# A decoder layer's cross-attention: exponentials of the second half per bank, one maximum over it, and probabilities kept as half-precision bit patterns

## The reference, cut to what matters

```python
q = (x @ Wq + bq).reshape(1, B * N, H, hd)          # 1024 queries
kv = (cond @ Wkv + bkv).reshape(1, -1, 2, H, hd)    # 2048 keys
k, v = (kv[:, :, 0], kv[:, :, 1])
...
q = _fq_sym(q, axis=-1)
k = _fq_sym(k, axis=-1)
v = _fq_sym(v, axis=2)
attn = jnp.einsum('bhqd,bhkd->bhqk', q, k)
attn = jax.nn.softmax(attn.astype(jnp.float32), axis=-1)
attn = _fq_unsigned(attn, axis=-1)    # step = row maximum / 255, rounded to 0..255 steps
out = jnp.einsum('bhqk,bhkd->bhqd', attn, v)
out = jnp.transpose(out, (0, 2, 1, 3)).reshape(B, N, C)
return out @ Wp + bp
```

## Time and profile before

| what | value |
|---|---|
| median of 3 runs | 1241.23 us (1237.27 to 1243.06) |
| the profiled execution, its own time | 1237.78 us |
| span of the profiled execution | 1236.1 us |
| `cross_scores`, first score matmul to last output copy | 399 to 871 us |
| busy over the whole span | PE 81%, DVE 69%, ACT 57%, POOL 20% |
| granted PE clock over the span | 0.95 of full speed |
| DMA inside `cross_scores` | nearly none: 0 to 3 GB/s in most slices |

### The profile page before, as it was taken

How to read it: one execution, slowest core, us unless ns; L and a number is a source line. 1 busy time by engine, 2 the same in 40 slices (tenths; PEclk the granted TensorE clock), 3 DMA queues, 4 the chain that set the end, 5 groups by cost and what they waited for, 6 DMA issues and landing times. The chain is left out here.

```text
span 1236.1 us, 21867 instructions
## 1 busy us (share of the span) xinstructions
PE 1003.9 (81%) x8049; PEld 682.7 (55%) x8049; DVE 852.8 (69%) x1409; ACT 700.4 (57%) x1039; POOL 243.6 (20%) x216
## 2 busy tenths in 40 slices
PE   4888996999457777777777777777779989999998
PEld 3745744888345444444444444444557765556566
DVE  6857546999687899999999999999661521111126
ACT  3453362455426899999999999999223202212221
POOL 1134063556250200000000000000533610000014
PEclk9999998999678799999999999999779989999999
DMA  8200004110000000000000000000040395131215
GB/s 320 96 1 1 1 2 154 51 34 17 9 0 13 31 1 2 1 0 0 0 0 0 0 0 0 0 0 0 1 151 27 135 379 230 60 116 64 69 56 182
DMA packets 24854, 68.14 MB, mean 55 GB/s; under 512 B 2722, under 2 KB 6818, under 8 KB 23778
## 3 DMA queue, kind: packets, MB, share of 16 engines
q1 hardware_dynamic: 20114, 52.48, 11.3%
q0 software_dynamic: 4400, 14.42, 3.7%
q10 hardware_dynamic: 288, 0.52, 0.1%
HBM read 49.07 MB, written 18.35 MB: 55 GB/s over the span
## 5 line engine op out<-in xcount | busy, mean ns | idle before, releaser
L1313 DVE TENSOR_REDUCE cs_top<-cs_s_b 128x1 f32<-128x512 f32 x256 | 164.8, 685 | 16.7 <-PE cs_s_b L1342 7.6
L1350 PE MATMUL cs_tp<-ident,cs_p_int 128*128 128x128 f16 x2048 | 158.4, 221 | 7.5 <-ACT cs_pT L1293 2.8
L1287 ACT ACTIVATE cs_p_int<-cs_s_b,cs_bias,cs_step_now 128x1024 int16<-128x1024 f32 x128 | 154.1, 1204 | 11.6 <-DVE cs_bias L1320 5.3
L1301 DVE TENSOR_REDUCE cs_top<-cs_s_a 128x1 f32<-128x1024 f32 x128 | 155.5, 1215 | 7.2 <-PE cs_s_a L1342 7.2
L1350 PEld LDWEIGHTS cs_tp<-ident,cs_p_int 128*128 128x128 f16 x2048 | 122.1, 98 | 60.3 <-issue 45.6
L1342 PE MATMUL cs_s_b<-k_parts,q_int 96*128 96x512 bf16 x256 | 79.0, 391 | 93.4 <-ACT cs_p_int L1287 93.1
L1287 ACT ACTIVATE cs_p_int<-cs_s_a,cs_bias,cs_step_now 128x1024 int16<-128x1024 f32 x128 | 152.8, 1194 | 0.0
L1293 ACT CAST cs_pT<-cs_tp 128x1024 bf16<-128x1024 int16 x128 | 129.5, 1012 | 3.3 <-PE cs_tp L1350 2.7
L2159 PE MATMUL ff_h<-ff_experts,ff_zgT 128*128 x368 | 115.1, 467 | 1.0 <-ACT ff_zgT L1798 0.9
L1446 POOL TENSOR_TENSOR co_o<-co_o,v_step 128x512 f32<-128x512 f32 x8 | 10.7, 1331 | 467.6 <-DVE co_o L1468 467.6
L1342 PE MATMUL cs_s_a<-k_parts,q_int 96*128 96x512 bf16 x256 | 79.4, 393 | 22.9 <-ACT cs_p_int L1287 18.7
(11 more groups left out here) (278 smaller groups left out, 2099.0 us busy)
## 6 DMA issues: line engine op xcount, KB each, us to landing
ff_experts<-in_experts_dram SPq DMA_DIRECT2D x8, 2176.0 KB, 14.6
slots<-sa_zero SPq DMA_DIRECT2D x1, 5888.0 KB, 25.8
ff_zg<-slots POOLq DMA_DIRECT2D x23, 256.0 KB, 2.9
run_y<-ff_yv SPq DMA_DIRECT2D x23, 256.0 KB, 2.0
ff_raw<-in_weights_dram SPq DMA_DIRECT2D x6, 768.0 KB, 5.8
ck_raw<-in_ctxT_dram SPq DMA_DIRECT2D x8, 512.0 KB, 3.3
stage<-in_cwkv_dram SPq DMA_DIRECT2D x2, 1024.0 KB, 6.8
out_dram<-x_res SPq DMA_DIRECT2D x8, 256.0 KB, 2.0
```

Of the source, the lines that this page charges most:

```text
L1287: nc.scalar.activation(p_int[:, u, half * HALF:(half + 1) * HALF], s[:, :], ACT.Exp, bias=bias[:, u:u + 1], scale=step_now[:, h:h + 1], ac ...
L1301: nc.vector.tensor_reduce(top[:, u, 0:1], s_a[u][:, :], AX_X, ALU.max).then_inc(max_ok, 1)
L1313: nc.vector.tensor_reduce(top[:, u, 1 + c:2 + c], s_b[:, c * 512:(c + 1) * 512], AX_X, ALU.max).then_inc(max_ok, 1)
L1350: ins = nc.tensor.transpose(tp[:, k, :], p_int[:, u, key:key + P].bitcast(F16), ident16[:, :])
```

## The change

It has five parts.

1. The exponential of half b is issued as two instructions of 512 keys, one for each bank (`PIECES = 3` sums per head instead of 2), and `eb_ok` is counted up by each. PE's score matmul for the first bank of the next unit waits for the first of them, that for the second bank for the second.
2. The maximum of half b is one instruction over 1024 values behind both score matmuls, in place of two instructions of 512, each behind its own.
3. The transposed probabilities stay bit patterns: `cs_pT` is int16, and L1376 (L1380 now) reads them as float16, in which the integer n is the subnormal number n * 2^-24. `v_int` becomes float16, and the copy of the output multiplies by 2^24 (`P_UNIT`).
4. ACT copies half b in pairs, as 512 int32 values instead of 1024 int16 ones. A pair is at most 255 * 65536 + 255, below 2^24. DVE copies half a as 1024 int16 values as before, to int16.
5. One exponential of a single column (`table`) stands ahead of the units on ACT.

The second score matmul now has a wait of its own. The diff, without the new declarations of constants and tiles that repeat part 3:

```diff
+            nc.scalar.activation(table[:, :], ident16[:, 0:1], ACT.Exp)
             units(act, step)
...
-                for half, s, made, used in ((1, s_b, eb_ok, tb_ok), (0, s_a[u], ea_ok, ta_ok)):
-                    if half:
+                for i, (first, count, s, made, used) in enumerate(((HALF, 512, s_b[:, 0:512], eb_ok, tb_ok),
+                                                                   (HALF + 512, 512, s_b[:, 512:HALF], eb_ok, None),
+                                                                   (0, HALF, s_a[u][:, :], ea_ok, ta_ok))):
+                    if i == 0:
                         act.wait_ge(bias_ok, n + 1)
-                    if at_least(n, 2):
+                    if used and at_least(n, 2):
                         act.wait_ge(used, n - 1)
-                    nc.scalar.activation(p_int[:, u, half * HALF:(half + 1) * HALF], s[:, :], ACT.Exp,
+                    nc.scalar.activation(p_int[:, u, first:first + count], s, ACT.Exp,
                                          bias=bias[:, u:u + 1], scale=step_now[:, h:h + 1],
-                                         accum_out=z_now[:, h, half:half + 1]).then_inc(made, 1)
+                                         accum_out=z_now[:, h, i:i + 1]).then_inc(made, 1)
...
-                nc.scalar.copy(pT[:, u, HKT:KT, :], tp[:, :, :].bitcast(I16)).then_inc(rb_ok, 1)
+                nc.scalar.copy(pT[:, u, HKT:KT, :].rearrange("p k q -> p (k q)").bitcast(I32),
+                               tp[:, :, :].rearrange("p k q -> p (k q)").bitcast(I32)).then_inc(rb_ok, 1)
...
-                    for c in range(2):
-                        v_.wait_ge(sb_ok, 2 * n + c + 1)
-                        nc.vector.tensor_reduce(top[:, u, 1 + c:2 + c], s_b[:, c * 512:(c + 1) * 512], AX_X,
-                                                ALU.max).then_inc(max_ok, 1)
-                    v_.wait_ge(max_ok, 3 * n + 3)
+                    v_.wait_ge(sb_ok, n + 1)
+                    nc.vector.tensor_reduce(top[:, u, 1:2], s_b[:, :], AX_X, ALU.max).then_inc(max_ok, 1)
+                    v_.wait_ge(max_ok, 2 * n + 2)
...
-                    nc.vector.tensor_copy(o_raw[:, t - 1, :], out[:, :]).then_inc(out_read, 1)
+                    nc.vector.tensor_scalar(o_raw[:, t - 1, :], out[:, :], P_UNIT, None, ALU.mult).then_inc(out_read, 1)
...
                 for c in range(2):
                     keys = half * HALF + c * 512
+                    if freed is not None:
+                        pe.wait_ge(eb_ok, freed + c)
...
-                    scores(t, h, s_b, 1, sb_ok, each_bank=True)
+                    scores(t, h, s_b, 1, sb_ok, freed=2 * n - 1 if at_least(n, 1) else None)
                 if before:
-                    pe.wait_ge(eb_ok, n)
+                    pe.wait_ge(eb_ok, 2 * n)
...
-                        ins = nc.tensor.matmul(out[:, head * D:(head + 1) * D], pT[:, u, k, :],
+                        ins = nc.tensor.matmul(out[:, head * D:(head + 1) * D], pT[:, u, k, :].bitcast(F16),
                                                v_int[:, k, head * D:(head + 1) * D], start=(k == 0), stop=(k == KT - 1))
```

More of the change, by code:

```diff
@@ L35 @@
 LN_PMAX = log(PMAX)
+P_UNIT = 2.0 ** 24
 Q_FLOOR = 1e-08
@@ L966 @@
 HALF = KEYS // 2
+PIECES = 3
 HKT = KT // 2
@@ L1198, in cross_scores @@
         p_int = sb("cs_p_int", [P, 2, KEYS], I16)
-        pT = sb("cs_pT", [P, 2, KT, P], BF16)
-        top = sb("cs_top", [P, 2, 3], F32)
+        pT = sb("cs_pT", [P, 2, KT, P], I16)
+        top = sb("cs_top", [P, 2, 2], F32)
         top1 = sb("cs_top1", [P, 2], F32)
@@ L1205, in cross_scores @@
         nstep_now = sb("cs_nstep_now", [P, H], F32)
-        z_now = sb("cs_z_now", [P, H, 2], F32)
+        z_now = sb("cs_z_now", [P, H, PIECES], F32)
         bias = sb("cs_bias", [P, 2], F32)
+        table = sb("cs_table", [P, 1], F32)
         s_a = [psum(f"cs_s_a{i}", [P, HALF], F32) for i in range(2)]
@@ L1338, in _, with scores @@
         def _(pe):
-            def scores(t, h, s, half, made, each_bank=False):
+            def scores(t, h, s, half, made, freed=None):
                 for c in range(2):
                     keys = half * HALF + c * 512
+                    if freed is not None:
+                        pe.wait_ge(eb_ok, freed + c)
                     ins = nc.tensor.matmul(s[:, c * 512:(c + 1) * 512], q_int[0:3 * D, t, h, :],
                                            k_parts[0:3 * D, h, keys:keys + 512], start=True, stop=True)
-                    if each_bank or c == 1:
-                        ins.then_inc(made, 1)
+                ins.then_inc(made, 1)
             def transposes(u, half, made):
@@ L1356, in step @@
                 if exists(n):
-                    if at_least(n, 1):
-                        pe.wait_ge(eb_ok, n)
-                    scores(t, h, s_b, 1, sb_ok, each_bank=True)
+                    scores(t, h, s_b, 1, sb_ok, freed=2 * n - 1 if at_least(n, 1) else None)
                 if before:
-                    pe.wait_ge(eb_ok, n)
+                    pe.wait_ge(eb_ok, 2 * n)
                     if at_least(n, 2):
@@ L1520, in cross_attention @@
         v_step = sb("v_step", [P, C], F32)
-        v_int = sb("v_int", [P, KT, C], BF16)
+        v_int = sb("v_int", [P, KT, C], F16)
         wq_raw = v_int[:, :, :].rearrange("p t c -> p (t c)")[:, 0:2 * CK * C].bitcast(F32)\
@@ L1538, in cross_attention @@
         bias = sb("bias_p", [P, C], F32)
-        z_sum = sb("z_sum", [P, TT, H, 2], F32)
+        z_sum = sb("z_sum", [P, TT, H, PIECES], F32)
         cross_scores(nc, k_parts, v_int, q_int, q_step, q_nstep, o_raw, z_sum, wp, bp, (w_raw, w_hi, w_lo, bias), ident16)
```

## The result

The changed kernel is slower: 1266.25 us as the median of four runs (1264.96 to 1267.34) against 1239.38 us of the kernel before (1237.27 to 1243.06, four runs). The ratio is 1.0213, with a 95% interval from 1.0182 to 1.0244. The forecast was 1267 us. The profiled execution took 1264.96 us, with a span of 1263.2; the sum had given 1264.3 and 1262.6.

What follows compares the result with a forecast made beforehand. The loop over `cs_s_b`, half b's single score buffer, was taken to bound. Repeats +33.5, tile joins -4.7, first units -0.8, table -1.3 gave about 26.5 us on 1237.8; with 3.4 to the median, 1267 us, range 1250 to 1281.

Steps and rivals of the forecast that it cites:

- The loop over `cs_s_b` bounds: Half b's single score buffer closes exponential, scores, maxima and bias into the bounding loop: 3.54 us, becoming 3.80.
- The split, 0.34: Half b's two narrow exponentials on the loop keep their fixed part and end at 1.54 instead of 1.20: +0.34 us a unit.
- B: Rival: a narrow exponential costs in proportion to width, so the split is free; near 1230 us, chance 3%.
- E: Rival: the second exponential overlaps its forerunner better, split costs 0.15 or less; 1241 to 1246 us, no change, chance 3%.
- C: Rival: the added exponential overlaps nothing, so the split costs 0.55 a unit; near 1294 us, chance 3%.
- A: Rival: ACT, the busiest engine, sets the pace, so -0.09 a unit counts; about 1228 us, chance 5%.
- The one maximum, -0.075: Half b's single maximum on the loop takes 1.215 us against 1.29 for the pair: -0.075 a unit.
- The first bank's earlier release buys nothing: Half b's first score matmul is ready early, but nobody can use it: no gain.
- The int32 copy, off the path: ACT's copy falls by 0.43 to 0.585 us, only deepening ACT's slack; at 1.012, parts between tiles would lose 3.8 us.
- The other loops stay below 3.80: Transposes of half a finish near 4.6, before DVE wants them at 4.81; ACT's loop is 3.30.
- Where tiles meet, -4.7: Between token tiles, new slack pays back 0.67 us, seven times: -4.7 us.
- case D: Rival: the PE clock falls as PE idles more, units take about 4.02; near 1301 us, chance 3%.

Runs made afterwards that it cites:

- e3: Changed kernel with half b's exponential whole again and its maximum as two instructions, one per bank; 1234.22 us, ratio 0.9938.
- e5: Changed kernel with ScalarE's copy as 1024 int16 values instead of 512 int32; 1271.82 us, ratio 1.0235.
- e2: Changed kernel, exponential still split, with half b's maximum again two instructions, each behind its own bank's matmul; 1237.84 us, ratio 0.9975.
- e4: Changed kernel with both score matmuls of half b waiting for the second exponential; 1312.37 us, ratio 1.0581.
- e6: As e2 (split exponential, two maxima), with ScalarE's copy as 1024 int16 values; 1255.42 us, ratio 1.0104.
- e7: As e2, with half a's maximum also two instructions, each behind its own matmul; 1228.57 us, ratio 0.9887.
- e1: Changed kernel with half b's exponential one instruction of 1024 again, the one maximum kept; 1253.72 us, ratio 1.0087.

## Why the prediction was right

Point by point, by its own steps:

- *The loop over `cs_s_b` bounds.* Right. Its parts in the changed kernel are 1.68 (both exponentials and the release), 0.43, 1.26 and 0.44: 3.81, forecast 3.80. That an engine's load was not the bound is shown by e3 and e5: 0.43 us less or more on ACT in each unit left the repeat at 3.54 and at 3.81.
- *The split, 0.34.* The narrow exponential took 772 ns (forecast 0.78) and the second began 0.77 behind the first (0.765); together they end 1.54 behind the bias, as forecast. The fixed part is kept, as the squares had shown; cases B and E (below 1.4) and C (above 1.65) are out, and A with them, since ACT is idle for 0.52 to 0.60 ahead of them. The 0.80 that the Trainium skill ("ScalarE: Activation LUTs", What ACT_TABLE_LOAD costs) gives for 512 elements was 0.03 too long for this one. The 0.36 that the prediction put beside it took the spacing of the two from the rows, so it is no test of the skill alone.
- *The one maximum, -0.075.* The instruction alone: 1.23 against 1.29, so -0.06. But the price named was only that of the instruction. Per bank the first would have started in the shadow of the second exponential, and e2 shows what is lost: 497.3 - 467.8 = 29.5 us of stage. With the whole exponential it is 485.0 - 465.1 = 19.9. So the prediction put the one maximum down as a small gain, and it is most of the loss.
- *"The first bank's earlier release buys nothing."* Wrong as put. Without it the repeat is 4.02 (e4), so it buys 0.21 a unit: it takes the first matmul out of the loop, and that is why the maximum could still start 0.43 behind a matmul. The sum was right since it counted 0.42 for that step; the sentence beside it was not.
- *The int32 copy, off the path.* Right in the changed kernel: 584 ns (forecast 585), and e5 costs 4.9 us of stage, of which 3.8 were forecast. The ACT loop that I gave for it was too long: by e6, ACT needs 3.62 with the 16-bit copy, where my way of adding gave 3.73.
- *The other loops stay below 3.80.* True here. PE had finished the transposes of half a 4.41 behind the exponential (forecast 4.6), 0.41 ahead of VectorE's copy. But one loop was missing from the list: the one over two units through half a, which e2 shows at 7.08. At 1.23 for the one maximum I estimate it at about 7.0 in the changed kernel, 3.5 a unit.
- *Where tiles meet, -4.7.* The four intervals around a join were 3.81, 4.09, 3.54 and 3.96 (15.40 in all) and are 3.98, 3.95, 3.81 and 3.89 (15.63). Four plain units would have added 1.08 and these add 0.23: -0.85 a join, -6.0. Of the 0.18 that the forecast of 0.67 lacks, 0.10 is the first interval, which I had left out.
- *The first two units, -0.8.* They took 4.18 and 4.19 and take 4.03 and 4.02. With +0.27 each as everywhere they would have taken 8.90 in all, so -0.85 is right. The third took 3.69 and takes 4.02. From 399.3 to 411.4 us the granted clock is 0.55. This bears on case D too: the prediction said 4.02 for a unit at the lower clock, which was right, but not for the reason beside it. The loop over `cs_s_b` takes 3.81 + 0.22 there, since its score matmul lasts 0.61 us, not 0.39; ACT's copy no longer closes the loop. Case D as a whole is out: the granted clock of the stage is 0.96, 0.97 from 460 to 850 us.
- *Not in the sum:* six units behind the first three took 4.02 or 4.03 instead of 3.81 (one of them, at a join, instead of 3.89), +1.2 in all. In the window of one of them (768.9 to 772.9 us) the granted clock is 0.60 and its score matmul lasts 0.61 us. A seventh took 4.06 at full clock; the kernel before had three longer units of its own, +0.7. From the first exponential to the last the stage grew by 28.0 us, just what 33.5 - 4.7 - 0.8 gives; but there the joins (-1.3 against the forecast) and the longer units cancel, and in the span the stages ahead (-3.9) and behind (+4.7) do. So the closeness of the total is in part luck; the repeat's is not. Nor is the 3.4 us from profile to median a fixed step: it is 1.3 in the changed kernel, and 1.6 in the one before with its fourth run.
- *The table, -1.3.* 1.35 less from the first maximum to the first exponential, of which some 0.07 is the maximum's. The drain of 1.38 that the Trainium skill (same page and section) adds to a switch shows in neither trace: the load ends at 396.39, and ACT's next instruction starts at 396.40.
- *The third sum.* The reduction behind the stage took 0.55 us, after 0.42: +0.13.

How the two central edits work together is what the sum had left out. In microseconds of stage, all with the int32 copy: whole with two maxima 465.1, split with two 467.8, whole with one 485.0, split with one 497.3. The split costs 2.7 with two maxima and 12.3 with one; the one maximum costs 19.9 without the split and 29.5 with it (by the medians 3.6, 12.5, 19.5 and 28.4). Together the two edits cost 9.6 more than their sum. With one maximum the early release of the first bank saves only its matmul's 0.21 (e4); with a maximum per bank the reading of that bank is taken out of the loop too. Even then the split did not pay by itself, since the loop over two units took its place.

## What to carry to other kernels

When two or three engines are each above 95% busy, don't ask which one is fullest but write down every loop that a buffer closes (who frees it, who fills it, who reads it, who waits for the reader) and add its parts; a buffer of two closes one over two repeats. If an instruction is split so that its pieces release banks early, split its consumers as well, or little more than the second fixed part is left; and look which loop bounds next, for here the split with both consumers of half b still lost 2.7 us, and only with maxima per bank in half a as well (e7) was a kernel with the split faster than the one without (e3). Before shortening an instruction, look whether its engine waits for another one right behind it: 0.43 us off the copy changed nothing in the repeat of the kernel before (e3), and was worth 14.7 us of the stage where ScalarE had become the bound (e6 to e2).

## What the runs showed of the hardware

- Most of the kernels with longer waits of PE had a lower granted TensorE clock. Between 460 and 850 us it was 1.00 in the kernel before and e3 (repeat 3.54), 0.97 in the changed kernel (3.81) and 0.82 in e4 (4.02 and 4.45). The repeat alone doesn't order them: e6 had 0.97 at 3.60 to 3.62, and e1 0.98 at 3.69. What makes it fall was not isolated. In e4 an added wait of 0.21 us a unit cost 27 us by itself and some 17 more, most of it in units at the lower clock.
- The duration that the profile gives an ACT instruction depends on what stands ahead of it: the same exponential of 512 shows 0.78 behind a wait (and 0.77 as the second of such a pair), and 0.90 in the stretch of e6 in which ACT never waits. The second starts 0.77 behind the first in the changed kernel and 0.76 in e6. Sums for a full engine are to be made from starts.
- ScalarE's copy of a PSUM bank as 512 int32 elements took 584 ns, as 512 float elements 585, as 1024 int16 elements 1012: the same bytes, so its time goes by elements here.
